# A two-layer GNN kernel: VectorE adds 0.01 z before ScalarE rectifies z in place in PSUM

## What is computed

```
def conv(x, src, dst, ea, Wm, We, Wr, b):
    msg = x[src] @ Wm + ea @ We
    agg = segment_max(msg, dst, 100000); agg = where(isneginf(agg), 0, agg)
    return agg + x @ Wr + b
c1 = leaky_relu(conv(x, src, dst, ea, W1m, W1e, W1r, b1))      # slope 0.01
c2 = leaky_relu(conv(c1, src, dst, ea, W2m, W2e, W2r, b2))
out = layernorm(x + c2)                                          # over 96 columns
```

## Time and profile before

| | |
|---|---|
| median of 3 runs | 1326.05 us (1324.7 to 1327.44) |
| profiled execution | 1329.25 us, of which the span of its trace is 1327.1 us |
| PE busy | 1023.8 us, 77% of the span |
| DVE busy | 811.1 us, 61% |
| ACT busy | 691.2 us, 52% |
| POOL busy | 989.1 us, 75% |
| mean granted TensorE clock | 0.736 of 2.4 GHz |

### The profile page before, as it was taken

How to read it: one execution, slowest core, us unless ns; L and a number is a source line. 1 busy time by engine, 2 the same in 40 slices (tenths; PEclk the granted TensorE clock), 3 DMA queues, 4 the chain that set the end, 5 groups by cost and what they waited for, 6 DMA issues and landing times.

```text
span 1327.1 us, 16475 instructions
## 1 busy us (share of the span) xinstructions
PE 1023.8 (77%) x4312; PEld 682.9 (51%) x4312; DVE 811.1 (61%) x1763; ACT 691.2 (52%) x1685; POOL 989.1 (75%) x986
## 2 busy tenths in 40 slices
PE   2666577778999999428888888887888889999900
PEld 1233233434666666216666665665666666666600
DVE  3223233326777777418777887777787787777720
ACT  1333244435666666305666666666666667666620
POOL 4777777775777777777777777777777777776775
PEclk9888888877555555558888888888898896555555
DMA  6888888877777777625555565655665635777420
GB/s 200 258 279 269 253 261 291 279 241 237 214 214 214 209 209 214 201 62 152 151 151 152 153 160 163 163 161 152 158 165 164 170 112 176 215 214 210 154 70 30
DMA packets 106083, 248.88 MB, mean 188 GB/s; under 512 B 26656, under 2 KB 27552, under 8 KB 105992
## 3 DMA queue, kind: packets, MB, share of 16 engines
q1 hardware_dynamic: 67432, 161.21, 41.0%
q0 software_dynamic: 31360, 48.23, 15.4%
q10 hardware_dynamic: 7200, 38.40, 7.4%
HBM read 141.94 MB, written 105.80 MB: 187 GB/s over the span
## 4 chain that ended last, share of the span: by engine, by line
PE 25%; ACT 14%; DVE 7%; issue 6%; POOL 4%; DMA 1%; POOLq 0%; DVEq 0%; SPq 0%; ACTq 0%
ACT yo L563 7%; PE ps L413 6%; PE ps_z L423 6%; POOL out L245 3%; PE ps_n L471 3%; PE ps_n L472 3%; PE ps_t L399 2%; ACT nat L625 2%; PE ps_m L403 2%; DVE yo L732 2%; PE ps_r L509 2%; DVE stat L743 2%; ACT c1d L648 1%; PE ps_r L511 1%; ACT c1t L537 1%
## 5 line engine op out<-in xcount | busy, mean ns | idle before, releaser
L423 PEld LDWEIGHTS ps_z<-wr,c1t 97*128 97x128 f32 x1568 | 302.6, 275 | 133.2 <-issue 89.8
L413 PE MATMUL ps<-xtb,wr 97*96 97x512 f32 x392 | 302.2, 866 | 0.0
L423 PE MATMUL ps_z<-wr,c1t 97*128 97x96 f32 x1568 | 298.1, 356 | 5.2 <-DVE c1t L725 5.2
L245 POOL DMA_INDIRECT agg_table<-nat,end_i x196 | 205.5, 1048 | 72.5 <-issue 56.2
L245 POOL DMA_INDIRECT out<-nat,end_i x196 | 205.4, 1048 | 63.8 <-issue 54.3
L563 ACT ACTIVATE yo<-yo,shift,rstd 128x96 f32<-128x96 f32 x654 | 243.8, 457 | 0.5 <-DVE shift L706 0.5
L235 POOL DMA_INDIRECT g_src<-in_x,src_i x196 | 187.5, 957 | 71.7 <-issue 58.2
L235 POOL DMA_INDIRECT g_dst<-in_x,own_i x196 | 195.5, 997 | 59.7 <-issue 59.7
L235 POOL DMA_INDIRECT g_src<-agg_table,src_i x196 | 194.5, 992 | 61.0 <-issue 58.8
L690 DVE TENSOR_TENSOR_SCAN mx<-mask,mx,ps_m 96x512 f32<-96x512 f32 x96 | 122.1, 1272 | 167.7 <-PE ps_m L403 167.7
L725 DVE TENSOR_TENSOR c1t<-ps,c1t 96x512 f32<-96x512 f32 x196 | 134.2, 685 | 78.4 <-ACT c1t L537 78.4
(11 more groups left out here) (58 smaller groups left out, 1198.4 us busy)
## 6 DMA issues: line engine op xcount, KB each, us to landing
xtb<-in_xt SPq DMA_DIRECT2D x98, 384.0 KB, 4.8
agg_table<-zero ACTq DMA_DIRECT2D x50, 750.0 KB
xn<-in_x SPq DMA_DIRECT2D x97, 384.0 KB, 3.2
out<-yo SPq DMA_DIRECT2D x97, 384.0 KB, 3.8
mask<-mask_row SPq DMA_DIRECT2D x98, 192.0 KB, 5.2
root_keep<-rt SPq DMA_DIRECT2D x49, 192.0 KB, 4.6
rt<-root_keep SPq DMA_DIRECT2D x49, 192.0 KB, 4.6
xe<-in_eat SPq DMA_DIRECT2D x98, 64.0 KB, 4.6
```

The lines of the kernel that those rows point to most:

```text
L245: nc.gpsimd.indirect_dma_start(out=rows, out_offset=bass.IndirectOffsetOnAxis(ap=end_i[:, t:t + 1], axis=0), in_=nat[:, t, :], in_offset=N ...
L413: nc.tensor.matmul(ps_1[0:D, h, :], wr1[:, :], xtb[:, k, half(h)], start=True, stop=True).then_inc(d_1, 1)
L423: last = nc.tensor.matmul(ps_z[:, h, row(j)], c1t[:, q % 2, cols(h * HJ + j)], wr2[:, :], start=True, stop=True)
```

## The change

DVE's `dense_u` now runs first, straight after PE's product, and no longer waits for ACT. ACT's `dense_r` waits for `dense_u` and writes relu(0.99 z) back into ps_z. DVE's `dense_y` adds ps_z and xn into yo, by halves of 384 columns. So ps_z is held until `dense_y`, and PE's next `layer2` waits for `dense_y` (d_y) where it waited for `dense_u` (d_u). The same is done for the edges: `edge_u`, `edge_r` in place in ps_n, `edge_y` with one operand from ps_n, and `sums_back` waits for e_y where it waited for e_u. `edge_y` and `edge_stats` are moved behind `dense_mid`. SP's next load into xn waits for both halves of y. The core of the diff:

```diff
 def layer2(q, h):                                   # PE
     pe.wait_ge(d_c1, 2 * q + h + 1)
-        pe.wait_ge(d_u, 2 * (q - 1) + h + 1)
+        pe.wait_ge(d_y, 2 * (q - 1) + h + 1)
 def sums_back(c):                                   # PE
-        pe.wait_ge(e_u, c)
+        pe.wait_ge(e_y, c)
 def dense_r(q, h):                                  # ACT
-    act.wait_ge(d_2, 2 * q + h + 1)
-    nc.scalar.activation(yo[:, q % YR, halfrow(h)], ps_z[:, h, 0:HJ * D],
+    act.wait_ge(d_u, 2 * q + h + 1)
+    nc.scalar.activation(ps_z[:, h, 0:HJ * D], ps_z[:, h, 0:HJ * D],
                          ACT.Relu, scale=1.0 - SLOPE).then_inc(d_r, 1)
 def edge_r(c):                                      # ACT
-    act.wait_ge(b_n, c + 1)
-    nc.scalar.activation(nat[:, c * TPC:(c + 1) * TPC, :], ps_n..., ACT.Relu, ...).then_inc(b_nc, 1)
+    act.wait_ge(e_u, c + 1)
+    nc.scalar.activation(ps_n[:, 0:TPC * D], ps_n[:, 0:TPC * D], ACT.Relu, ...).then_inc(b_nc, 1)
 def dense_u(q, h):                                  # DVE
-    dve.wait_ge(d_r, 2 * q + h + 1)
+    dve.wait_ge(d_2, 2 * q + h + 1)
-def dense_y(q):
-    dve.wait_ge(d_u, 2 * q + 2)
-    t = yo[:, q % YR, :]
-    V.tensor_tensor(t, t, xn[:, q % XR, :], ALU.add).then_inc(d_y, 1)
+def dense_y(q, h):
+    dve.wait_ge(d_r, 2 * q + h + 1)
+    V.tensor_tensor(yo[:, q % YR, halfrow(h)], ps_z[:, h, 0:HJ * D], xn[:, q % XR, halfrow(h)],
+                    ALU.add).then_inc(d_y, 1)
 def dense_tail(steps):
-        dense_y(d - 1)
+        dense_y(d - 1, 0)
+        dense_y(d - 1, 1)
         dense_stats(d - 1)
 # DVE, stage B, chunk c
     if 1 <= c <= NCH:
+        edge_u(c - 1)
+    dense_mid(steps)
+    if 1 <= c <= NCH:
         edge_y(c - 1)
         edge_stats(c - 1)
-    dense_mid(steps)
```

More of the change, by code:

```diff
@@ L309, in load_pair @@
                 if q >= XR:
-                    sp.wait_ge(d_y, q - XR + 1)
+                    sp.wait_ge(d_y, 2 * (q - XR) + 2)
                 if q < NQ - 1:
@@ L542, in dense_r @@
                     return
-                act.wait_ge(d_2, 2 * q + h + 1)
-                if q >= YR and h == 0:
-                    act.wait_ge(o_st[q % YR], 16 * (q // YR))
-                nc.scalar.activation(yo[:, q % YR, halfrow(h)], ps_z[:, h, 0:HJ * D],
+                act.wait_ge(d_u, 2 * q + h + 1)
+                nc.scalar.activation(ps_z[:, h, 0:HJ * D], ps_z[:, h, 0:HJ * D],
                                      ACT.Relu, scale=1.0 - SLOPE).then_inc(d_r, 1)
@@ L605, in edge_r @@
             def edge_r(c):
-                act.wait_ge(b_n, c + 1)
[L607 to L611, removed]
+                act.wait_ge(e_u, c + 1)
+                nc.scalar.activation(ps_n[:, 0:TPC * D], ps_n[:, 0:TPC * D],
                                      ACT.Relu, scale=1.0 - SLOPE).then_inc(b_nc, 1)
@@ L725, in dense_c1 @@
                 V.tensor_tensor(t, ps_1[0:D, h, :], t, ALU.max).then_inc(d_c1, 1)
-            def dense_y(q):
+            def dense_y(q, h):
                 if not real(q):
                     return
-                dve.wait_ge(d_u, 2 * q + 2)
-                t = yo[:, q % YR, :]
-                V.tensor_tensor(t, t, xn[:, q % XR, :], ALU.add).then_inc(d_y, 1)
+                dve.wait_ge(d_r, 2 * q + h + 1)
+                if q >= YR and h == 0:
+                    dve.wait_ge(o_st[q % YR], 16 * (q // YR))
+                V.tensor_tensor(yo[:, q % YR, halfrow(h)], ps_z[:, h, 0:HJ * D], xn[:, q % XR, halfrow(h)],
+                                ALU.add).then_inc(d_y, 1)
             def dense_stats(q):
@@ L736, in dense_stats @@
                     return
-                dve.wait_ge(d_y, q + 1)
+                dve.wait_ge(d_y, 2 * q + 2)
                 if q >= 2:
@@ L804, in edge_scale, with edge_u @@
                                        in1=erstd[:, c % 2, :], op0=ALU.mult, op1=ALU.mult).then_inc(e_shift, 1)
-            def edge_y(c):
-                dve.wait_ge(b_nc, c + 1)
+            def edge_u(c):
+                dve.wait_ge(b_n, c + 1)
                 dve.wait_ge(l_dst[c % RD], 64 * (c // RD) + 64)
@@ L811, in edge_y @@
                                        op0=ALU.mult, op1=ALU.add).then_inc(e_u, 1)
-                dve.wait_ge(e_u, c + 1)
-                t = nat[:, c * TPC:(c + 1) * TPC, :]
-                V.tensor_tensor(t, t, u.rearrange("p (r d) -> p r d", r=TPC), ALU.add).then_inc(e_y, 1)
+            def edge_y(c):
+                dve.wait_ge(b_nc, c + 1)
+                if c == 0:
+                    for k in range(2):
+                        dve.wait_ge(sc_t[k], 64 * ((NCH + 1 - k) // 2))
+                V.tensor_tensor(nat[:, c * TPC:(c + 1) * TPC, :],
+                                ps_n[:, 0:TPC * D].rearrange("p (r d) -> p r d", r=TPC),
+                                g_dst[:, c % RD, :].rearrange("p (r d) -> p r d", r=TPC),
+                                ALU.add).then_inc(e_y, 1)
             def edge_stats(c):
```

## The result

The changed kernel takes 1498.63 us (median of 3 runs, 1498.11 to 1500.89) where the kernel before takes 1326.05: a ratio of 1.129, 95% interval 1.127 to 1.131, slower by 172 us. The profiled execution is that of 1498.11 us, and its span is 1496.3 us.

What follows compares the result with a forecast made beforehand. POOL, the longest chain, was taken to bound the kernel. Dense and edge chain: +30 (S), +109 (B), +52 (tail), less 39 of cover, is +152 us, POOL's saving buying nothing: 1480 us, range 1434 to 1535.

Steps and rivals of the forecast that it cites:

- POOL's saving: POOL's transfers: no longer stretched by DVE adds of two SBUF operands, 50 us less, between 40 and 58.
- The loop in S and the tail: Stage S and tail: `layer2` waits for `dense_y`, 2.1 us later every turn, 6.72 becomes 8.8 us.
- Stage B: Stage B: four terms sum to 6.8 us per three chunks, low 4.0, high 9.4; 16 times, +109 us.
- rectify and t1 in series at the head: Head of B's dense chunks: c1 waits for u, r and t1 in series, 1.0 us twice, 2.0 per three chunks.
- `layer2` behind c1d and the sum, and the clock: B: `layer2` and `layer1` delay `sums_back` in a dense chunk behind a dense one, 3.0 us; half clock 1.0.
- the edges' sum moved and in PSUM: B's chunk without a pair: u, r, ACT's copy and part of the moved sum before the scan, 0.8 us.
- the `dense_mid` half: Second dense half in B: costs nothing new, since ACT's list already orders r and t1 there.
- the rival with a falling clock: Stage B: PE's idle keeps its clock at half for most of B, +60 us more, 1540; chance 0.12.
- The tail and the cover: Tail: 24 turns add 50 us and two pairs 2, +52; 39 us of cover at the end comes off.
- POOL staying the bound: Rival: POOL remains the bound and its 50 us come off, 1276; chance 0.04.
- swallow its waits: Rival: stage B absorbs the added waits, leaving +43 us, 1369; chance 0.05.
- The clock did not rise: Rival: PE's clock rises in S and the tail, a turn takes 7.35 us, 1365 up to 1400; chance 0.05.

Runs made afterwards that it cites:

- Run 8: The changed kernel with both halves of dense_y on DVE ahead of dense_c1(d, 1), and the edges as in the kernel before: 1291.90 us, ratio 0.972.
- Run 6: The changed kernel with both dense_y halves ahead of dense_c1(d, 1), dense_r writing to yo in SBUF and dense_y adding yo and xn: 1331.98 us against 1327.68.
- Run 9: The kernel before with one line changed, layer2 on PE waiting for d_y (the whole sum) in place of d_u: 1488.15 us against 1330.45, ratio 1.119.
- run 10: The kernel before with only the edges' part of the change: 1350.51 us, ratio 1.015.
- run 7: The changed kernel with both halves of dense_y moved on DVE ahead of dense_c1(d, 1): 1319.40 us, ratio 0.992 to the kernel before.
- run 12: The kernel before with dense_y as two adds of 384 columns right behind each other, both operands in SBUF: 1854.29 us against 1822.34 on a slow chip.
- run 1: The kernel before with layer2 on PE waiting for d_y (the whole sum) in place of d_u, on a slow chip: 2027.76 us against 1820.54.
- run 4: The kernel before with only the edges' part of the change, on a slow chip: 1874.53 us against 1820.54, ratio 1.029.

## Why the prediction was right, and where its steps were off

**What bounded the kernel, and POOL's saving.** Right. POOL's busy time fell by 52.1 us (predicted 50), and it bought nothing in the changed kernel. Run 8 adds what the prediction could not have: 41 us when PE keeps up. The part of the reasoning that was too simple is what makes the stretch: not two SBUF operands alone, but above all their being in one long instruction. Run 6 has the operands and 17 us, the operands in one long sum and 52.

**The loop in S and the tail.** Right in its place and nearly in its size: `layer2` 2.1 us late every turn, measured 448.43 - (444.56 + 1.71) = 2.16. The term was mis-sized in two ways. The eight products that start after a wait take longer: from 448.43 to 450.22 is 1.79 us, where it was 1.65 without a wait, so the turn grows by 2.30 and not 2.1. And the old stage S began with a few turns of 5 to 6.4 us at the full clock, so that 34 turns took 226.4 us and not 34 x 6.72; the new ones are 9.02 from the start. Over 34 turns that is 80 us instead of 72, and another 2 lie ahead of them; PE leaves S 82 us later, and with the 41.91 of idle taken off B starts 40 us late, not 30. Run 9 shows that this wait alone does it.

**Stage B.** The sum was right, 12.7 us per chunk predicted and 12.63 measured, but its terms were not all so. The runs without standstills give, per three chunks:

| part | predicted | measured | from |
|---|---|---|---|
| rectify and t1 in series at the head | 2.0 | 0.0, net of the sums' earlier place | run 8 against before, 10.48 and 10.48 |
| `layer2` behind c1d and the sum, and the clock | 3.0 + 1.0 | 4.4, with the longer sum | run 9, 3 x (11.94 - 10.48) |
| the edges' sum moved and in PSUM | 0.8 | 1.9 | run 10, 3 x (11.12 - 10.48) |
| all | 6.8 | 6.4 | the change, 3 x (12.63 - 10.48) |

The edges' term was mis-sized, 0.8 for 1.9 (run 7 less run 8 gives 2.1). It was put at a chunk without a pair; in the turn of run 7 shown above it is a wait that the edges' sum no longer fills, in a chunk with one. The measured parts add up to 6.3, but no run has the head's series alone: run 8 puts 1.5 and 0.9 us on the dense chunks, near the predicted 2.0, and takes 2.9 off the third. Whether the changed kernel, with its sums late, gets that back, no run shows. Nor was the `dense_mid` half free, as the prediction had it: in the changed kernel DVE's second c1 waits 2.89 us for ACT's t1 at 909.45, and over B all 66 c1 wait, 110.3 us in sum, for 0.3 in the kernel before. Part of this is hidden in c1d's own wait for ACT, which falls from 77.4 to 32.1 us. So the mechanism was right, and that the sum came out within half a microsecond is in part luck.

The bounds of B were also added up wrongly. The high ends of the four terms make 10.4 us and not 9.4, the low ones 4.2 and not 4.0. The range's upper end of 1535 goes with 10.4; with the 150 us that stand beside it, it would be 1519. The measured time lies within either.

The wait of a dense chunk behind a dense one is the longest in the changed kernel. PE's rows, and c1d's in between:

```profile
905.08 1.02 PE L413 MATMUL ps<-xtb,wr 97*96 97x512 f32 x2
...
912.88 0.75 DVE L860 SCALAR_TENSOR_TENSOR c1d<-ps_r,b1c,c1d 96x512 f32<-96x512 f32 x1 [0.44 <-ACT c1d L642]
913.55 1.01 DVE L727 TENSOR_TENSOR yo<-ps_z,xn 128x384 f32<-128x384 f32 x2
914.24 1.99 PE L423 MATMUL ps_z<-wr,c1t 97*128 97x96 f32 x8 [4.67 <-DVE yo L727]
...
916.03 1.91 PE L413 MATMUL ps<-xtb,wr 97*96 97x512 f32 x2
...
917.74 0.58 PE L471 MATMUL ps_n<-wr,c1d 97*128 97x96 f32 x2
```

c1d is ready for `sums_back` at 913.6, and `sums_back` starts at 917.74 behind `layer2` and `layer1`. Behind 4.67 us of idle these two run at the lower clock level, 0.50: 1.91 where `layer1` took 1.02 at 905.08, at 1.00. From 913.6 to 917.74 is 4.1 us, the case that the prediction had put at 3.9 for the half clock. The mean clock between B's first and last c1d fell from 0.89 to 0.82, so the rival with a falling clock had the right sign and a small part of its size. How much of the 4.4 is clock and how much is waiting, no run separates.

**The tail and the cover.** Predicted +52 and measured +63 from B's last c1d: 24 turns of 2.3 make 55, and the two pairs in B's last turns cost more than the 2 that I gave them. The cover at the end was 39.6 us, as predicted. The sum, 152 us for the 169.2 between the spans, came out 17 us too low, by 13 up to B's first c1d and 11 behind B, less 6 in B.

**The rivals.** POOL staying the bound needed PE's new wait to be hidden; it was 1.96 us a turn. B did not swallow its waits: its chunk grew by 2.15 us. The clock did not rise: S stayed at 0.50 with PE busy 235 of 300 us, as it does with PE busy 229 of 230 (run 7). No run supports a cause outside the order of DVE's list.

## What to carry to other kernels

When a change makes a buffer's last reader another instruction, look where that instruction stands in its engine's list, and at what stands ahead of it there: here one wait behind a c1 that itself needs PE's last product cost 12%, and moving two adds up by one place turned the change into a gain. Price what it frees on another engine separately, since it may be worth all or nothing depending on this order. And break a forecast that came out right into its terms by runs of one part each: in B one term was less than half of what it turned out to be, and another, put at nothing, was a wait of up to 2.89 us.

## What the runs showed of the hardware

- A DVE add of two SBUF operands takes 0.945 us for 768 columns and, for 384, 0.557 (run 6) or 0.546 where two follow each other (run 12): 1.01 to 1.04 ns a column and 0.15 to 0.17 us for each instruction. With one operand in PSUM 384 columns take 0.544 to 0.552, so PSUM costs nothing here.
- An indirect transfer on POOL that meets such an add grows from 0.96 to as much as 2.4 us where the add has 768 columns, and to no more than 1.5 where it has 384. Over 980 transfers the long adds cost 52 us in the kernel before (35 in run 1, 59 in run 10), the short ones 9 to 17.
- On three of the five chips the same program took 34 to 37% longer. In stretches there, the engine that first reads a product of PE started about 19 us after it had ended, with nothing else to wait for in the code (run 4), and the DMA engines moved 60 GB/s, for 204. Why those chips do so stays open. No run there says which kernel is better on a chip without the standstills.
- TensorE's granted clock was 0.50 for 300 us with PE busy 235, and for 230 us with PE busy 229 (run 7), while in B it fell to that level behind an idle of 4.67 us. The Trainium skill (TensorE: Matmul & The Clock Gate, What's actually happening) has the lower level as the idle state; B agrees, S does not.
